# Preparing the slot weights inside the drain of cross attention, with the second pair copied by GpSimd

## The chip, the cores and the metric

The kernel runs on one core of one Trainium2 chip. The metric is the device time of one execution in microseconds (us), lower is better. The program's parts run on TensorE (PE), VectorE (DVE), ScalarE (ACT) and GpSimd (POOL), and SyncE (SP) issues most DMAs.

## The reference

64 sequences of 128 tokens with 128 features go through three sub-layers, each with a residual and a layer norm: self attention, cross attention over 77 context tokens, and a soft mixture of 64 experts with 32 slots each. Only the last one reads what the change touches:

```python
logits = (einsum('tzd,ed->tze', x, phi_w) + phi_b).reshape(t, z, 64, 32)
D = softmax(logits, axis=3)            # over the 32 slots of an expert
C = softmax(logits, axis=2)            # over the 64 experts
X_tilde = einsum('tznp,tzd->npd', D, x)          # gather
X_tilde = tanh(normalise(clip(X_tilde)))
Y_tilde = einsum('npd,ndH->npH', X_tilde, expert_w) + expert_b
Y = einsum('tznp,npH->tzH', C, Y_tilde)          # mix
```

## The kernel before, in words

`decoder_block` runs seven stages one behind the other, each a function with its own block of instruction streams: `setup`, `attention`, `attend_context`, `prepare_slots`, `gather_slots`, `run_experts`, `mix_slots`. A stage begins on every engine after all engines have ended the one before it.

`attend_context` (L380 to L739) takes 64 batches of 128 tokens through a software pipeline, `STEPS = range(-4, B + 4)`. In step n an engine works on batch n (scores), n-1 (exponentials), n-2 (values, sums, division), n-3 (output projection, residual, statistics, normalisation) and n-4 (transposition to `xh` and `xl`). The order of each engine is written out by hand in its loop over STEPS. The steps after B - 1 = 63 are the drain: no new scores, and each step has fewer parts. The names that matter there, by engine:

- PE: `values` L547, `project` L503, `sums` L553, `turn_x2` L508.
- ACT: `exponentials` L596, which reads the four PSUM banks of `psP` (`cross_P`) and raises `e_ready`; the copy to `xh` at L619, which waits for `turn_x2`.
- DVE: `add_residual` L656 to L658, `aggregate` L663, `low_part` L678, `normalise` L668, `invert_sums` L674, `divide` L684.
- POOL: `own_keys` L721, then `normalise` with L727, L730 and L732.

`prepare_slots` (L742 to L791) turns `phi` (2048 slot vectors of 128 features, held with the bias) into the weights of the logits. DVE subtracts from the first 127 features the last one and puts the bias in its place (`diff`, L766 and L769), PE transposes 16 blocks of 128x128 into four PSUM banks (L781), ACT writes the rounded high part `w1h` (L790) and, reordered from (expert, slot) to (slot, expert) and for slots 0 to 15 only, `w2h` (L791), and DVE writes the rests `w1l` (L774) and `w2l` (L775). It works in four chunks of 512 columns. `w1h` and `w1l` are read by the gather stage, `w2h` and `w2l` by the mix stage alone (L1159).

`gather_slots` (L794 to L945) begins with a DMA of the expert weights and one of the expert bias on SP's queue (L837, L838); the stores of kept logits (L841) stand behind them on the same queue, and ACT's `keep` tiles, three of them, are free again when their store has landed (L879). Its steady part takes 128 units, each with L942 and L936 on POOL. `run_experts` (L948 to L1080) begins on DVE with clips (L979), on PE with transposes, and on POOL with nothing until the first statistics are there: L1016 waits for `mv_ready`, L1018 makes `rstd`, and DVE's L994 waits for that. `mix_slots` runs over 64 tiles.

The memory of x1T (the transposed output of self attention, 32 KB in each partition) is kept until the end of `attend_context`; its last reader is the projection of the last pair of batches, `queries_keys` L485, whose semaphore is `qk_made`.

Of the kernel before, what the change touches and what calls it, by code (L numbers as in the profile page):

```python
# [18 lines left out]
ALU = mybir.AluOpType  # L19
# [360 lines left out]
def attend_context(nc, io, w):  # L380
# [4 lines left out]
    with ExitStack() as ctx:  # L385
# [18 lines left out]
        xp = [st.sb(f"xp{i}", [128, 128]) for i in range(2)]  # L404
        halves = nc.dram_tensor("cross_halves", (2, 2, 128, WIDE), F32, kind="Internal").ap()
        psS = st.ps("S", [128, 2, 512])
        psP = st.ps("P", [J, 4, 4, 128])
        psO = st.ps("O", [128, 2, 128])
        psM = st.ps("M", [128, 512])
        QUERY, KEY = slice(0, 256), slice(256, WIDE)  # L410
# [10 lines left out]
        pj_made, y_done, st_done, mv_ready, ve_done, rstd_ready, x2_ready, x2_kept, xT_made, xh_ready, xl_ready = (  # L421
            st.sem(n) for n in ("pj_made", "y_done", "st_done", "mv_ready", "ve_done", "rstd_ready", "x2_ready",
                                "x2_kept", "xT_made", "xh_ready", "xl_ready"))
        pack_set, consts_set, vd_clear, od_set = (st.sem(n) for n in ("pack_set", "consts_set", "vd_clear", "od_set"))
        block = ctx.enter_context(nc.Block())
        PACKS = 6 * 16
# [2 lines left out]
        def is_batch(n):  # L429
            return 0 <= n < B  # L430
# [43 lines left out]
        def _(pe):  # L474
# [75 lines left out]
            def sums(n, part):  # L550
# [4 lines left out]
                if part == 1:  # L555
                    ins.then_inc(av_made, 1)

            for n in STEPS:
                if n == 0:
                    pe.wait_ge(consts_set, 1)  # L560
                if n == 2:
                    pe.wait_ge(od_set, 4)
                if is_batch(n):
                    scores(n, 0)
                for r in projected(n):
                    queries_keys(r)
                for r in valued(n):
                    own_values(r)
                if is_batch(n - 2):
                    values(n - 2, 0)  # L570
                if is_batch(n):
                    scores(n, 1)
                if is_batch(n - 2):
                    values(n - 2, 1)
                if is_batch(n - 3):
                    project(n - 3)
                if is_batch(n - 2):
                    sums(n - 2, 0)
                if is_batch(n - 4):
                    turn_x2(n - 4)  # L580
                if is_batch(n):
                    turned_scores(n)
                    turn_max(n)
                if is_batch(n - 2):
                    sums(n - 2, 1)
                if is_batch(n):
                    shift(n)

        @block.scalar
        def _(act):  # L590
            def exponentials(n, half):
                if half == 0:
                    act.wait_ge(t_made, n + 1)
                    reach(act, av_made, n - 1)
                hs = slice(2 * half, 2 * half + 2)
                ins = act.activation(pT[n % 2][0:J, hs, :, :], psP[:, hs, :, :], ACT.Exp)  # L596
                if half == 1:
                    ins.then_inc(e_ready, 1)

            for n in STEPS:  # L600
                if n == 1:
                    act.wait_ge(od_set, 4)
                if is_batch(n - 1):
                    exponentials(n - 1, 0)
                for r in projected(n):
                    act.wait_ge(qk_made, r + 1)
                    reach(act, stored, 16 * r)
                    act.copy(qk[:, 0, :], psM[:, 0:WIDE]).then_inc(high_ready, 1)
                for r in valued(n):
                    act.wait_ge(v_made, r + 1)  # L610
                    act.wait_ge(vd_clear, 1)
                    reach(act, av_made, 2 * r - 4)
                    act.copy(blocks(vd[r % 3][0:J]), psM[0:J, 0:256].rearrange("j (c h e) -> j c h e", c=8, h=4))\
                        .then_inc(vd_ready, 1)
                if is_batch(n - 1):
                    exponentials(n - 1, 1)
                if is_batch(n - 4):
                    act.wait_ge(xT_made, n - 3)
                    act.copy(w.xh[:, tokens(n - 4)], psM[:, 0:128]).then_inc(xh_ready, 1)  # L619
                if is_batch(n):  # L620
                    act.wait_ge(m_made, n + 1)
                    reach(act, t_made, n)
                    act.copy(mT[:], psM[:, 0:128]).then_inc(mT_ready, 1)

        @block.vector
        def _(dve):
# [54 lines left out]
            def divide(n):  # L681
                dve.wait_ge(rs_ready, n + 1)
                reach(dve, pj_made, n - 1)
                dve.tensor_tensor(oT[n % 2][:], psO[:, 0, :], rs[:], ALU.mult).then_inc(oT_ready, 1)  # L684

            for n in STEPS:
                if n == -3:
                    clear_values()
                if is_batch(n):
                    peak(n, 0)  # L690
                for r in projected(n):
# [5 lines left out]
                    aggregate(n - 3)  # L697
                if is_batch(n - 4):
                    low_part(n - 4)
                if is_batch(n - 3):  # L700
                    normalise(n - 3)
                if is_batch(n - 2):
                    invert_sums(n - 2)
                    divide(n - 2)

        @block.gpsimd
        def _(pool):
# [27 lines left out]
            for n in STEPS:  # L735
                if is_batch(n + 1):
                    own_keys(n + 1)
                if is_batch(n - 3):
                    normalise(n - 3)  # L739


def prepare_slots(nc, w):  # L742

    with ExitStack() as ctx:
        st = Store(nc, ctx, "prep")  # L750
        diff = st.sb("diff", [128, 16, 128])
        psW = st.ps("W", [128, NP])
        diff_done, w_made, wh_done = (st.sem(n) for n in ("diff_done", "w_made", "wh_done"))
        block = ctx.enter_context(nc.Block())

        def by_slot(t, c):

            return t[:].rearrange("d (p n) -> d n p", n=EXPERTS)[:, 16 * c:16 * c + 16, :]

        def by_expert(t, c):  # L760
            return t[:, c * 512:(c + 1) * 512].rearrange("d (n p) -> d n p", n=16)[:, :, 0:MADE]

        @block.vector
        def _(dve):
            dve.wait_ge(w.phi_loaded, 32)
            dve.tensor_copy(diff[:, :, 127], w.bias[:])  # L766
            for c in range(4):
                p = slice(4 * c, 4 * c + 4)
                dve.tensor_tensor(diff[:, p, 0:127], w.phi[:, p, 0:127], w.phi[:, p, 127:128].to_broadcast([128, 4, 127]),  # L769
                                  ALU.subtract).then_inc(diff_done, 1)  # L770
            for c in range(4):
                b = slice(c * 512, (c + 1) * 512)
                dve.wait_ge(wh_done, c + 1)
                dve.tensor_tensor(w.w1l[:, b], psW[:, b], w.w1h[:, b], ALU.subtract)  # L774
                dve.tensor_tensor(by_slot(w.w2l, c), by_expert(psW, c), by_slot(w.w2h, c), ALU.subtract)  # L775

        @block.tensor
        def _(pe):
            for c in range(16):
                pe.wait_ge(diff_done, c // 4 + 1)  # L780
                ins = pe.transpose(psW[:, c * 128:(c + 1) * 128], diff[:, c, :], w.ident)  # L781
                if c % 4 == 3:
                    ins.then_inc(w_made, 1)

        @block.scalar
        def _(act):
            for c in range(4):
                b = slice(c * 512, (c + 1) * 512)
                act.wait_ge(w_made, c + 1)
                act.copy(w.w1h[:, b], psW[:, b])  # L790
                act.copy(by_slot(w.w2h, c), by_expert(psW, c)).then_inc(wh_done, 1)  # L791


def gather_slots(nc, io, w, psX):  # L794
# [153 lines left out]
def run_experts(nc, w, psX):  # L948
# [5 lines left out]
    with ExitStack() as ctx:  # L954
# [55 lines left out]

        @block.gpsimd
        def _(pool):
            for c in range(4):
                p = slice(4 * c, 4 * c + 4)
                pool.wait_ge(mv_ready, c + 1)
# [261 lines left out]
def decoder_block(nc, io, out):  # L1277
    with ExitStack() as ctx:
        st = Store(nc, ctx, "kept")
        w = Weights()  # L1280
        w.xres = st.sb("xres", [128, TOKENS])
        w.xh = st.sb("xh", [128, TOKENS], F32R)
        w.xl = st.sb("xl", [128, TOKENS], F32R)
# [14 lines left out]
        w.bias = st.sb("bias", [128, 16])  # L1298
        with ExitStack() as first:
            sf = Store(nc, first, "first")  # L1300
            w.x1T = sf.sb("x1T", [128, TOKENS])
            w.m, w.w2a, w.b2 = sf.sb("m", [128, 128]), sf.sb("w2a", [128, 129]), sf.sb("b2", [128, 128])
            w.cvec, w.beta = sf.sb("cvec", [128, 1]), sf.sb("beta", [128, 1])
            w.xq, w.xqs, w.xo = sf.sb("xq", [128, 128]), sf.sb("xqs", [128, 128]), sf.sb("xo", [128, 128])
# [4 lines left out]
            w.fill_by_batch, w.fill = fill, fill.rearrange("(r b) t -> r (b t)", b=2)  # L1309
            setup(nc, io, w)  # L1310
            attention(nc, io, w)
            attend_context(nc, io, w)
        w.yk = w.phi
        w.kept = nc.dram_tensor("kept_logits", (TOKENS, 2, SLOTS - MADE, 32), F32, kind="Internal").ap()
        w.w2h, w.w2l = st.sb("w2h", [128, EXPERTS * MADE], F32R), st.sb("w2l", [128, EXPERTS * MADE], F32R)
        with ExitStack() as banks:
            sl = Store(nc, banks, "slots")
            psX = sl.ps("X", [128, 4, 512])
            w.we = sl.sb("we", [128, EXPERTS, 128])
            w.beT = sl.sb("beT", [128, EXPERTS])  # L1320
            with ExitStack() as second:
                ss = Store(nc, second, "second")
                w.w1h, w.w1l = ss.sb("w1h", [128, NP], F32R), ss.sb("w1l", [128, NP], F32R)
                prepare_slots(nc, w)
                gather_slots(nc, io, w, psX)
            run_experts(nc, w, psX)
        mix_slots(nc, w, out)

# [30 lines left out]
```

## Time and profile before

| | us |
|---|---|
| median of 3 runs | 1541.6 |
| lowest and highest run | 1538.96, 1542.17 |
| the profiled execution's own time | 1542.46 |
| its span in the profile | 1540.7 |

| engine | busy us | share of the span |
|---|---|---|
| PE (matmul) | 1395.6 | 91% |
| DVE | 1174.1 | 76% |
| POOL | 1151.4 | 75% |
| ACT | 870.2 | 56% |

The times in the profile count from the span's start. A busy share is an average over stages with different limits, so what matters here is read from the stretches around the change.

### The profile page before, as it was taken

The page shows a single profiled execution, that of the slowest core. Times are in us where ns is not written, and L with a number is a line of the kernel's source. Part 1 is how long each engine was busy: PE and PEld are TensorE (multiplying, and loading weights), DVE is VectorE, ACT ScalarE, POOL GpSimd, SP SyncE. Part 2 cuts the span into 40 slices and gives each one's busy share as a digit, 9 for nine tenths or more (in the row PEclk, how much of TensorE's full clock was granted, in tenths as well). Part 3 has the DMA queues.
Part 4 walks back from the last instruction along what each step waited for, and adds up shares of the span by engine and source line. Part 5 has one row for each costly group of instructions (what it writes and reads, how often), then busy time and mean ns, then how long its engine had stood idle before and what let it go on. Part 6 is the DMA issues. An engine that isn't in the chain of part 4 may idle for free. (4 is left out here: it accounts for less than half of the span.)

```text
span 1540.7 us, 35158 instructions
## 1 busy us (share of the span) xinstructions
PE 1395.6 (91%) x12926; PEld 1111.6 (72%) x12926; DVE 1174.1 (76%) x2389; ACT 870.2 (56%) x1546; POOL 1151.4 (75%) x1028
## 2 busy tenths in 40 slices
PE   5765699999999985999999999996999999999998
PEld 4554466666666653777777777764999999999998
DVE  4898477777777765888888888885788787787885
ACT  3677244444444433667677677662565665656655
POOL 2343466666666642999999999992899999999997
PEclk9897599999999997999999999998999999999999
DMA  5110342323333304222222222211222232232230
GB/s 159 35 35 13 98 118 90 90 90 94 97 94 103 91 19 137 79 80 75 82 77 75 83 76 78 81 69 54 75 87 78 84 94 79 77 93 79 77 93 29
DMA packets 77196, 123.82 MB, mean 80 GB/s; under 512 B 8354, under 2 KB 45795, under 8 KB 77027
## 3 DMA queue, kind: packets, MB, share of 16 engines
q1 hardware_dynamic: 75426, 117.16, 23.9%
q0 software_dynamic: 1088, 4.19, 0.9%
q8 instruction: 104, 1.70, 0.5%
q14 instruction: 66, 0.53, 0.1%
q10 hardware_dynamic: 512, 0.23, 0.1%
HBM read 70.28 MB, written 51.27 MB: 79 GB/s over the span
## 5 line engine op out<-in xcount | busy, mean ns | idle before, releaser
L942 POOL TENSOR_TENSOR gather_d<-gather_e,gather_rinv 128x1024 f32<-128x1024 f32 x128 | 245.0, 1914 | 53.2 <-DVE gather_rinv L921 53.2
L1248 POOL TENSOR_TENSOR mix_c<-mix_e,mix_rinv 128x1024 f32<-128x1024 f32 x128 | 241.0, 1904 | 24.7 <-DVE mix_rinv L1215 24.7
L1175 PEld LDWEIGHTS mix_Y<-kept_phi,mix_cT 128*128 128x128 f32 x2048 | 248.1, 192 | 9.0
L1175 PE MATMUL mix_Y<-kept_phi,mix_cT 128*128 128x128 f32 x2048 | 249.0, 275 | 0.0
L1191 ACT COPY mix_cT<-mix_T 128x1024 f32<-128x1024 f32 x128 | 128.7, 1005 | 170.0 <-PE mix_T L1182 170.0
L1212 DVE TENSOR_REDUCE mix_sums<-mix_e 128x16 f32<-128x1024 f32 x128 | 152.6, 1192 | 85.3 <-ACT mix_e L1195 83.0
L917 DVE TENSOR_REDUCE gather_rsum<-gather_e 128x32 f32<-128x1024 f32 x128 | 156.2, 1220 | 26.9 <-ACT gather_e L890 26.9
L721 POOL TENSOR_TENSOR cross_kd<-cross_pack,kept_consts 128x624 fp32r<-128x624 f32 x128 | 155.3, 1233 | 23.4 <-DMA cross_pack<-cross_halves 23.4
L936 POOL TENSOR_TENSOR gather_dl<-gather_d,gather_dh 128x512 fp32r<-128x512 f32 x128 | 166.1, 1298 | 0.0
L596 ACT ACTIVATE cross_pT<-cross_P 77x1024 f32<-77x1024 f32 x128 | 130.4, 1022 | 48.3 <-PE cross_P L536 48.3
L879 ACT COPY gather_keep<-gather_L 128x256 f32<-128x256 f32 x256 | 94.7, 370 | 105.3 <-PE gather_L L853 98.7
L1182 PE MATMUL mix_T<-kept_consts,mix_c 128*128 128x128 f32 x1024 | 134.6, 275 | 5.1 <-POOL mix_c L1248 5.0
L1259 POOL TENSOR_TENSOR mix_less<-mix_read,mix_high 128x1024 f32<-128x1024 f32 x64 | 122.5, 1915 | 19.5 <-DVE mix_high L1228 19.2
L890 ACT ACTIVATE gather_e<-gather_L 128x1024 f32<-128x1024 f32 x128 | 131.2, 1025 | 8.3 <-PE gather_L L860 1.0
L649 DVE TENSOR_REDUCE cross_mx<-cross_S 128x8 fp32r<-128x624 f32 x128 | 102.9, 804 | 36.8 <-PE cross_S L518 36.7
L867 PE MATMUL slots_X<-gather_d,kept_xres 128*128 128x512 f32 x256 | 130.9, 593 | 0.0
L1182 PEld LDWEIGHTS mix_T<-kept_consts,mix_c 128*128 128x128 f32 x1024 | 117.5, 143 | 6.5 <-POOL mix_c L1248 6.5
L911 DVE TENSOR_REDUCE gather_mx<-gather_L 128x16 fp32r<-128x512 f32 x128 | 88.5, 691 | 33.0 <-PE gather_L L853 24.1
L727 POOL TENSOR_TENSOR cross_veps<-cross_mv,kept_eps 128x1 f32<-128x1 f32 x64 | 12.2, 190 | 128.8 <-DVE cross_mv L663 128.8
L872 PE MATMUL slots_X<-gather_dh,gather_x2h 128*128 128x512 f32 x128 | 101.3, 792 | 2.9 <-DVE gather_x2l L927 1.5
L902 ACT CAST gather_dh<-gather_d 128x512 fp32r<-128x512 f32 x128 | 79.7, 623 | 32.1 <-PE slots_X L874 20.3
L853 PE MATMUL gather_L<-second_w1h,kept_xh 128*128 128x512 f32 x256 | 82.0, 401 | 12.4 <-ACT gather_e L890 8.7
(188 smaller groups left out, 3168.2 us busy)
## 6 DMA issues: line engine op xcount, KB each, us to landing
kept_logits<-gather_keep SPq DMA_DIRECT2D x128, 256.0 KB, 2.0
mix_read<-kept_logits SPq DMA_DIRECT2D x64, 512.0 KB, 3.7
cross_halves<-cross_qk SPq DMA_DIRECT2D x32, 412.0 KB, 3.0
cross_pack<-cross_halves SPq DMA_DIRECT2D x64, 128.0 KB
cross_pack<-cross_halves SPq DMA_DIRECT2D x32, 206.0 KB
cross_pack<-cross_halves SPq DMA_DIRECT2D x64, 78.0 KB
attn_xTg<-in_xT SPq DMA_DIRECT2D x16, 256.0 KB, 2.7
kept_xres<-in_x POOLq DMA_DIRECT2D x4, 1024.0 KB, 12.0
```

The source lines that it names most:

```text
L596: ins = act.activation(pT[n % 2][0:J, hs, :, :], psP[:, hs, :, :], ACT.Exp)
L721: pool.tensor_tensor(kd[n % 2][:, q], keys[:, q].to_broadcast([128, 2, 4, JP]), w.own.unsqueeze(1).unsqueeze(3).to_broadcast([128, 2, 4, J ...
L867: pe.matmul(psX[:, 2 * j + 1, :], w.xres[:, rows(u)], dd[u % 4][:, 1, :], start=first, stop=last)\
L890: act.activation(e[u % 2][:], psL[u % 2][:].rearrange("p i (n s) -> p i n s", n=16), ACT.Exp)\
L917: dve.tensor_reduce(rsum[u % 2][:].rearrange("p (i n) -> p i n", i=2), e[u % 2][:], X, ALU.add)\
L936: pool.tensor_tensor(dl[u % 2][:], dd[u % 4][:, 0, :], dh[u % 2][:], ALU.subtract).then_inc(dl_ready, 1)
L942: pool.tensor_tensor(dd[u % 4][:].rearrange("p i (n s) -> p i n s", n=16), e[u % 2][:], rinv[u % 2][:].rearrange("p (i n) -> p i n", i=2). ...
L1175: ins = pe.matmul(psY[t % 2][:, 0:128], cT[u % 2][:, c, :], w.yk[:, 8 * (u % 2) + c, :], start=(u % 2 == 0 and c == 0), stop=(u % 2 == 1 a ...
L1182: ins = pe.transpose(psT[:, c, :], cc[u % 2][:, 2 * c:2 * c + 2, :], w.ident)
L1191: act.copy(cT[u % 2][:], psT[:]).then_inc(cT_ready, 1)
L1212: dve.tensor_reduce(sums[u % 2][:], e[u % 2][:], X, ALU.add).then_inc(sum_done, 1)
L1248: pool.tensor_tensor(cc[u % 2][:], e[u % 2][:], rinv[u % 2][:].unsqueeze(2).to_broadcast([128, 16, EXPERTS]), ALU.mult)\
```

## The change

The stage `prepare_slots` is gone. Its subtractions, transposes, and the writing of `w1h` and `w1l` are put into the streams of `attend_context`, in steps 63 to 67. The tiles `w1h`, `w1l`, `w2h`, `w2l` and `diff` take the memory of x1T. The transposes write to the four banks of `psP`. `w2h` and `w2l` are no longer made from PSUM by ACT and DVE: POOL copies them, reordered, from `w1h` and `w1l` at the beginning of `run_experts`.

```diff
@@ attend_context @@
-        psP = st.ps("P", [J, 4, 4, 128])
+        banks = st.ps("P", [128, 4, 4, 128])
+        psP = banks[0:J]
+        psW = banks[:].rearrange("d i q t -> d (i q t)")
...
+        diff_done, w_made, wh_done = (st.sem(n) for n in ("diff_done", "w_made", "wh_done"))
@@ tensor @@
+            def turn_weights(c):
+                pe.wait_ge(diff_done, c + 1)
+                pe.wait_ge(e_ready, B)
+                for p in range(4 * c, 4 * c + 4):
+                    ins = pe.transpose(psW[:, p * 128:(p + 1) * 128], w.diff[:, p, :], w.ident)
+                ins.then_inc(w_made, 1)
             for n in STEPS:
...
                 if is_batch(n):
                     shift(n)
+                if n == B:
+                    turn_weights(0)
+                    turn_weights(1)
+                if n == B + 1:
+                    turn_weights(2)
+                    turn_weights(3)
@@ scalar @@
+            def weights_high(c):
+                b = slice(c * 512, (c + 1) * 512)
+                act.wait_ge(w_made, c + 1)
+                act.copy(w.w1h[:, b], psW[:, b]).then_inc(wh_done, 1)
             for n in STEPS:
                 if n == 1:
                     act.wait_ge(od_set, 4)
+                if n == B + 1:
+                    weights_high(0)
+                    weights_high(1)
+                if n == B + 2:
+                    weights_high(2)
+                    weights_high(3)
@@ vector @@
+            def differences(chunks):
+                for c in chunks:
+                    p = slice(4 * c, 4 * c + 4)
+                    dve.tensor_tensor(w.diff[:, p, 0:127], w.phi[:, p, 0:127],
+                                      w.phi[:, p, 127:128].to_broadcast([128, 4, 127]), ALU.subtract)\
+                       .then_inc(diff_done, 1)
+            def weights_low(c):
+                b = slice(c * 512, (c + 1) * 512)
+                dve.wait_ge(wh_done, c + 1)
+                dve.tensor_tensor(w.w1l[:, b], psW[:, b], w.w1h[:, b], ALU.subtract)
             for n in STEPS:
                 if n == -3:
                     clear_values()
+                if n == B + 3:
+                    weights_low(2)
...
                 if is_batch(n - 4):
                     low_part(n - 4)
+                if n == B + 2:
+                    weights_low(1)
                 if is_batch(n - 3):
                     normalise(n - 3)
                 if is_batch(n - 2):
                     invert_sums(n - 2)
                     divide(n - 2)
+                if n == B - 1:
+                    dve.wait_ge(qk_made, PAIRS)
+                    dve.wait_ge(w.phi_loaded, 32)
+                    dve.tensor_copy(w.diff[:, :, 127], w.bias[:])
+                    differences((0, 1))
+                if n == B:
+                    differences((2, 3))
+                if n == B + 1:
+                    weights_low(0)
+                if n == B + 3:
+                    weights_low(3)
@@ prepare_slots: the whole function is removed @@
@@ run_experts, gpsimd @@
+            for low, high in ((w.w1h, w.w2h), (w.w1l, w.w2l)):
+                pool.tensor_copy(high[:].rearrange("d (p n) -> d n p", n=EXPERTS),
+                                 low[:].rearrange("d (n p) -> d n p", n=EXPERTS)[:, :, 0:MADE])
             for c in range(4):
                 p = slice(4 * c, 4 * c + 4)
                 pool.wait_ge(mv_ready, c + 1)
@@ decoder_block @@
-            w.x1T = sf.sb("x1T", [128, TOKENS])
+            w.x1T = x1T_space.enter_context(nc.sbuf_tensor("first_x1T", [128, TOKENS], F32, side="right"))
...
             attention(nc, io, w)
-            attend_context(nc, io, w)
+            x1T_space.close()
+            over = lambda name, shape: ctx.enter_context(nc.sbuf_tensor(f"over_{name}", shape, F32R, side="right"))
+            w.w1h, w.w1l = over("w1h", [128, NP]), over("w1l", [128, NP])
+            w.w2h, w.w2l = over("w2h", [128, EXPERTS * MADE]), over("w2l", [128, EXPERTS * MADE])
+            with nc.sbuf_tensor("over_diff", [128, 16, 128], F32, side="right") as w.diff:
+                attend_context(nc, io, w)
...
-                prepare_slots(nc, w)
-                gather_slots(nc, io, w, psX)
+            gather_slots(nc, io, w, psX)
```

## Rows read from the trace of the kernel before

**Rows 1.** Busy time by stretch; columns: stretch, length, engines, PEclk, DMA share, GB/s.

```profile
584.00:592.00 8.00, 3.49 (x17) 3.28 (x17) 7.11 (x13) 3.85 (x8) 0.00 (x0) 0.71 0.00 0
592.00:598.00 6.00, 6.00 (x14) 4.38 (x14) 1.84 (x3) 1.12 (x3) 0.00 (x0) 0.50 0.74 223
...
611.00:616.00 5.00, 4.85 (x11) 3.51 (x12) 2.86 (x4) 2.29 (x6) 3.13 (x2) 0.58 0.14 52
```

**Rows 2.** Timeline of preparation: start, duration, engine and line, names, count, [idle before].

```profile
584.09 2.47 DVE L769 TENSOR_TENSOR prep_diff<-kept_phi 128x508 f32<-128x508 f32 x4
...
585.98 0.59 ACT L790 CAST second_w1h<-prep_W 128x512 fp32r<-128x512 f32 x1 [2.62 <-PE prep_W L781]
...
590.43 0.71 DVE L774 TENSOR_TENSOR second_w1l<-prep_W,second_w1h 128x512 fp32r<-128x512 f32 x1
591.03 0.62 DVE L775 TENSOR_TENSOR kept_w2l<-prep_W,kept_w2h 128x256 fp32r<-128x256 f32 x1
...
591.99 0.74 SPq L837 DMA_DIRECT2D slots_we<-in_expert_w  x1
```

**Rows 3.** Timeline of cross attention's drain, DVE.

```profile
571.49 0.29 DVE L656 TENSOR_TENSOR cross_y<-cross_M,kept_xres 128x128 f32<-128x128 f32 x1 [1.68 <-PE cross_M L503]
...
576.50 0.29 DVE L656 TENSOR_TENSOR cross_y<-cross_M,kept_xres 128x128 f32<-128x128 f32 x1 [1.68 <-PE cross_M L503]
...
580.40 0.29 DVE L656 TENSOR_TENSOR cross_y<-cross_M,kept_xres 128x128 f32<-128x128 f32 x1 [0.58 <-PE cross_M L503]
...
581.47 0.29 DVE L678 TENSOR_TENSOR kept_xl<-cross_M,kept_xh 128x128 fp32r<-128x128 f32 x1 [0.23 <-ACT kept_xh L619]
...
582.19 0.35 DVE L668 TENSOR_SCALAR cross_xp<-cross_y,cross_mv,cross_rstd 128x127 f32<-128x127 f32 x1 [0.42 <-POOL cross_rstd L730]
...
583.40 0.29 DVE L678 TENSOR_TENSOR kept_xl<-cross_M,kept_xh 128x128 fp32r<-128x128 f32 x1 [0.87 <-ACT kept_xh L619]
```

**Rows 4.** Timeline of the same drain, PE, ACT and POOL.

```profile
572.41 0.19 POOL L727 TENSOR_TENSOR cross_veps<-cross_mv,kept_eps 128x1 f32<-128x1 f32 x1 [3.68 <-DVE cross_mv L663]
...
574.96 1.08 PE L547 MATMUL cross_O<-cross_pT,cross_vd 128*32 128x128 f32 x32 [2.10 <-DVE cross_oT L684]
...
577.33 0.27 ACT L619 CAST kept_xh<-cross_M 128x128 fp32r<-128x128 f32 x1 [4.74 <-PE cross_M L508]
...
579.88 0.49 PE L503 MATMUL cross_M<-first_xo,cross_oT 128*128 128x128 f32 x2 [2.01 <-DVE cross_oT L684]
...
581.17 0.27 ACT L619 CAST kept_xh<-cross_M 128x128 fp32r<-128x128 f32 x1 [3.58 <-PE cross_M L508]
```

**Rows 5.** Timeline of the experts' end, PE: transposes at the full clock.

```profile
1065.17 1.97 PE L1038 MATMUL expert_T<-kept_consts,expert_xt 128*128 128x128 f32 x16 [0.78 <-DVE expert_xt L1006]
```

**Rows 6.** One line's instructions, L927 on DVE: ns min/median/max.

```profile
L927 DVE TENSOR_TENSOR gather_x2l<-kept_xres,gather_x2h x64: 227/228/1305, 604.1 to 1036.4; 128x128 fp32r<-128x128 f32 x64
```

**Rows 7.** Timeline of the gather stage's start, SP's queue and ACT.

```profile
592.78 12.57 SPq L838 DMA_DIRECT2D slots_beT<-in_expert_bT  x1
...
609.80 0.37 ACT L879 COPY gather_keep<-gather_L 128x256 f32<-128x256 f32 x1 [6.18 <-DMA kept_logits<-gather_keep]
```

**Rows 8.** Timeline of the experts' start, DVE and POOL.

```profile
1043.70 2.48 DVE L979 TENSOR_SCALAR expert_xt<-slots_X 128x512 f32<-128x512 f32 x4 [5.95 <-PEq L802]
...
1047.47 0.20 POOL L1016 TENSOR_TENSOR expert_veps<-expert_mv,kept_eps 128x4 f32<-128x4 f32 x1 [5.49 <-DVE expert_mv L988]
...
1048.82 1.36 DVE L994 TENSOR_SCALAR expert_n<-expert_T,expert_mv,expert_rstd 128x128 f32<-128x128 f32 x4 [0.23 <-POOL expert_rstd L1018]
```

**Rows 9.** Groups of POOL's instructions: line, names, shapes, count, busy us, mean ns, idle.

```profile
L942 POOL TENSOR_TENSOR gather_d<-gather_e,gather_rinv 128x1024 f32<-128x1024 f32 x128 | 245.0, 1914 | 53.2 <-DVE gather_rinv L921 53.2
...
L732 POOL TENSOR_SCALAR kept_xres<-cross_y,cross_mv,cross_rstd 128x128 f32<-128x128 f32 x64 | 55.3, 865 | 6.7
...
L713 POOL MEMSET cross_pT<- 64x2048 f32 x2 | 4.0, 2016 | 0.1
```

More of the change, by code:

```diff
@@ L739, in _ @@
                     normalise(n - 3)
[L742 to L791, printed above, removed]
 def gather_slots(nc, io, w, psX):
@@ L1280, in decoder_block @@
         w = Weights()
+        x1T_space = ExitStack()
         w.xres = st.sb("xres", [128, TOKENS])
@@ L1311, in decoder_block @@
             attention(nc, io, w)
-            attend_context(nc, io, w)
+            x1T_space.close()
[4 more added lines that the diff above has]
+                attend_context(nc, io, w)
         w.yk = w.phi
         w.kept = nc.dram_tensor("kept_logits", (TOKENS, 2, SLOTS - MADE, 32), F32, kind="Internal").ap()
-        w.w2h, w.w2l = st.sb("w2h", [128, EXPERTS * MADE], F32R), st.sb("w2l", [128, EXPERTS * MADE], F32R)
         with ExitStack() as banks:
@@ L1320, in decoder_block @@
             w.beT = sl.sb("beT", [128, EXPERTS])
-            with ExitStack() as second:
-                ss = Store(nc, second, "second")
-                w.w1h, w.w1l = ss.sb("w1h", [128, NP], F32R), ss.sb("w1l", [128, NP], F32R)
-                prepare_slots(nc, w)
-                gather_slots(nc, io, w, psX)
+            gather_slots(nc, io, w, psX)
             run_experts(nc, w, psX)
```

## The prediction

> **What bounds the kernel at this place.** I read three views in this order. First the busy time by stretch. Between 584 and 592 us, the whole of `prepare_slots`, no engine has the work of another stage beside it: DVE is busy for 7.11 of 8 us, PE for 3.49, POOL for none [rows 1]. So the stage stands fully in the path, and what shortens the way from the last work of cross attention to the first of the gather shortens the kernel. Second the timeline of this stage and of the drain before it, engine by engine. DVE's last cross instruction starts at 583.40 and ends at 583.69 [rows 3]; DVE's last preparation ends at 591.65, and SP issues the gather's first DMA at 591.99 [rows 2]. From the one to the other: 8.30 us. In the drain the rows' idle times are the room into which the change puts its work. Third the start of the gather, because it decides whether an earlier start is kept. SP's queue is held by the two loads of expert weights for 12.57 us, to 605.35; the stores of kept logits stand behind them, and ACT waits 6.18 us for one of them, until 609.80 [rows 7]. This wait is counted from the moment SP issues the first load, so it moves forward with it. An earlier issue is kept in full; a faster PE before the wait is not worth anything.
>
> **Removed.** The 8.30 us from 583.69 to 591.99.
>
> **Added to the drain, by engine.** *DVE, subtractions.* Four took 2.47 us [rows 2], two take 1.24; with the bias column, of the order of 0.1, the first pair wants 1.35 us and the second 1.24. The first stands behind the division of step 63, in an idle time of 1.68 us before 571.49; the second behind the division of step 64, in one of 1.68 before 576.50 [rows 3]. Cost nothing; without that cover 2.6 us.
>
> *PE, transposes.* Sixteen at the full clock took 1.97 us [rows 5], eight take 1.0. They stand at the end of steps 64 and 65, in idle times of 2.10 us before 574.96 and 2.01 before 579.88 [rows 4]. Their inputs are in time: the second pair of subtractions ends at about 576.1, before the sums of step 65 are done. What they must not overtake, `e_ready` of the last batch, is raised before ACT's idle time of 4.74 us that ends at 577.33 [rows 4]. Cost nothing; uncovered 2.0 us.
>
> *ACT, high parts.* 0.59 us each [rows 2], two per step, 1.2 us. The first two follow the transposes (about 573.9) and lie in the 4.74 us before 577.33; the other two follow those of step 65 (about 578.9) and lie in the 3.58 us before 581.17 [rows 4]. Queued behind them is only the next copy to `xh`, which came later anyway. Cost nothing; uncovered 2.4 us.
>
> *DVE, low parts.* One lasts 0.71 us, and the next queued instruction starts 0.60 after it [rows 2]. Four places. (0) behind the division of step 65, in 0.58 us of idle time before 580.40: nothing, at most 0.1. (1) before the normalisation of batch 63, which had 0.42 us of idle time before 582.19 [rows 3]: 0.60 - 0.42 = 0.18 at most; I take 0.15. Behind it waits the chain normalisation, transposition, `xh`, `low_part`, which ends the stage. (2) in the 0.87 us before 583.40 [rows 3]: nothing. (3) behind the last `low_part`, with nothing to cover it: 0.60 to 0.70. So cross attention's DVE ends at 583.69 + 0.15 + 0.6 to 0.7, about 584.45. The step to the next stage took 591.99 - 591.65 = 0.34 us [rows 2]; SP's first load goes out at 584.8, against 591.99. **Gain of this part: 7.2 us**, between 7.0 and 7.4.
>
> *The port that DVE and POOL share.* One DVE subtraction with both inputs in SBUF took 1305 ns where its median is 228 [rows 6]; in the timeline it began while POOL was in a subtraction of its own. The new DVE subtractions of `diff` have both inputs in SBUF too. They would be held by at most one POOL instruction of 865 ns [rows 9]. But POOL is idle for 3.68 us before 572.41 [rows 4], which holds the first pair, and in the same way before its next batch. The low parts read PSUM and one SBUF tile. I take nothing.
>
> By the Trainium skill (SBUF — State Buffer, Who interferes with whom) a DVE instruction with two SBUF inputs and a GpSimd one that reads SBUF exclude each other for a whole instruction. The 1305 ns agree with it. By this rule a meeting of DVE's `diff` with L732 would cost up to 0.87 us, less the 0.3 to 0.4 us left of the gap, and the order of instructions keeps them apart.
>
> **Moved to POOL.** Two copies of 128x1024 elements between SBUF tiles, reordered on writing (runs of 16 read, written 64 elements apart). No copy on POOL is in the trace. Below: it can't gain, since POOL issues nothing else earlier for it; at the rate of its memset, 2016 ns for 2048 elements [rows 9], one takes 1.0 us. Above: at the rate of L732, 865 ns for 128 elements, 6.9 us. The nearest row is L942, 1024 elements with two inputs, read from and written to SBUF: 1.91 us [rows 9]. A copy has one input fewer, so I take 1.5 us, and 1.9 as its near bound: 3.0 to 3.8 us for both. The cover: the experts' stage starts at 1043.70 and POOL has nothing until 1047.47, 3.77 us [rows 8]. **Cost taken: nothing.** If they last longer, the rest is paid in full: behind them wait L1016 and `rstd`, and DVE's normalisation had only 0.23 us of idle time for it [rows 8]. DVE's instructions beside the copies read PSUM or one small tile, so I expect none of them held.
>
> **Sum.** Profiled execution 1542.46 - 7.2 = 1535.3, a span of 1533.5. The median of the runs is 0.9 below that execution, so I forecast 1541.6 - 7.2 = **1534.4 us**. About 0.2%, 3.1 us, is what a measurement of this kernel can tell from no change.
>
> **The rivals.**
> *Copies beyond their cover* (this is the one on the other side). Place: POOL at the start of the experts; price: what two copies last less 3.77 us. At 3.9 us each the gain falls under 3.1 us, at 5.5 us it is gone, from 7.0 us on the kernel is slower by over 0.2%. At the rate of L732 it is 13.8 - 3.77 = 10.1, for 1544.5. For it: the scattered writing, and that L732 shows how slow POOL can be per element. Against it: L732 has two operations with a scalar for each partition and only 128 elements over which to spread its start, and L942 has 1.87 ns an element. A milder form: the scattered access makes an element half as dear again as in L942, 2.9 us a copy, 2.0 us beyond the cover, for 1536.4; that is the likeliest within this case, 0.07. Chance in all 0.18: 0.09 still faster, 0.06 same, 0.03 slower.
>
> The Trainium skill's GPSIMD Engine Reference (Performance pitfalls for Q7 kernels) has such a rule, which speaks against this part: reading with a step over 8 bytes costs about 2.9 in place of 1.9 cycles per element. The copies read with step 1 and write with a step of 256 bytes, on which the page says nothing, and no row here shows it either way.
>
> *The drain does not hide it.* The waits could chain (DVE's difference late, then the transposes, then the projection of batch 62 or 63 queued behind them on PE). If all of it is paid, 2.6 of subtractions, 2.0 of transposes and DVE's four low parts of 0.6 come to 7.0 us in place of 8.3 us (ACT's high parts beside them, as in the stage itself), a gain of 1.3: 1540.3. Half hidden: 1537.5. For it: gaps of 1.68 us for 1.35 and 0.58 for 0.60 are narrow. Against it: each addition stands behind that step's last instruction and its inputs are a step old. Chance 0.10: 0.03 faster, 0.06 same, 0.01 slower.
>
> *TensorE's clock moves too.* It is at 1.2 GHz throughout the gather's first 6 us and at 0.58 of full on the mean from 611 to 616, when the units resume after the wait for the store [rows 1]; before both PE had been idle. The first stretch costs nothing, since the DMA wait swallows it. The second does: PE is busy for 4.85 us there, and at 2.4 GHz it would be some 2 us less, for 1532.4. The resuming comes after an equal idle time, so I expect the same. Chance 0.04.
>
> **How the numbers follow.** Forecast 0.68, copies 0.18, drain 0.10, clock 0.04. Faster: 0.68 + 0.09 + 0.03 + 0.04 = 0.84; same 0.12; slower 0.04. The range goes down to the clock's case less 0.8 us for the spread of the runs (1542.17 - 1538.96), 1531.6, and up to copies of some 4 us each, 1538.6.
>
> **What would show it.** In the profile after: SP's first load at 584.8; DVE's last low part starting at about 583.7; project of batch 63 still at 579.9 and normalisation within 0.2 us of 582.2; ACT's `keep` wait of about 6 us as before, ending at 602.6; two POOL copies of 1 to 2 us from about 1036.5, and L1016 within 4 us of the experts' start; the stretch from there to the end as long as before. Wrong: a first load later than 585.5 (the drain), a DVE wait for `rstd` over 0.5 us (the copies), a gather or mix stage of another length (what I have not seen).

## The result, and the profile after

Three comparisons were made of the changed kernel with the kernel before. The second and third are among the experiments below (labels e2_after_again and e9_after_third).

| comparison | before, median us | after, median us | ratio, 95% interval |
|---|---|---|---|
| first | 1541.88 | 1529.15 (6 runs, 1528.4 to 1532.79) | 0.9929, 0.9918 to 0.9939 |
| second | 1541.05 | 1531.74 (4 runs) | 0.9944, 0.9927 to 0.9961 |
| third | 1540.88 | 1532.42 (5 runs) | 0.9950, 0.9936 to 0.9964 |

The forecast was 1534.4 in a range of 1531.6 to 1538.6. The gain was 12.7 us in the first comparison, and 9.3 and 8.5 in the others; over all 15 runs the median is 1531.7, against 1541.3 over all 91 of the kernel before, 9.6 us. The direction was right and the size too small: the first result lies some 2.5 us below the range, and the median of all runs 0.1 us inside it.

The first profile of the changed kernel has a span of 1526.9 us in an execution of 1528.72. Its timeline of the drain (start, duration, engine and line, names, count, idle before), which answers to [rows 2 to 4]:

```profile
565.32 1.28 DVE L716 TENSOR_TENSOR over_diff<-kept_phi 128x508 f32<-128x508 f32 x2
...
569.77 1.09 PE L565 MATMUL cross_P<-kept_consts,over_diff 128*128 128x128 f32 x8
...
574.21 1.09 PE L565 MATMUL cross_P<-kept_consts,over_diff 128*128 128x128 f32 x8
...
574.90 1.07 ACT L619 CAST over_w1h<-cross_P 128x512 fp32r<-128x512 f32 x2 [0.89 <-PE cross_P L565]
...
576.16 0.68 DVE L723 TENSOR_TENSOR over_w1l<-cross_P,over_w1h 128x512 fp32r<-128x512 f32 x1
576.29 0.30 PEld L506 LDWEIGHTS cross_M<-first_xo,cross_oT 128*128 128x128 f32 x2 [1.23 <-DVE cross_oT L711]
...
576.82 0.29 DVE L683 TENSOR_TENSOR cross_y<-cross_M,kept_xres 128x128 f32<-128x128 f32 x1
...
578.10 0.68 DVE L723 TENSOR_TENSOR over_w1l<-cross_P,over_w1h 128x512 fp32r<-128x512 f32 x1
...
578.70 0.34 DVE L695 TENSOR_SCALAR cross_xp<-cross_y,cross_mv,cross_rstd 128x127 f32<-128x127 f32 x1
578.95 0.68 DVE L723 TENSOR_TENSOR over_w1l<-cross_P,over_w1h 128x512 fp32r<-128x512 f32 x1
...
579.75 0.29 DVE L705 TENSOR_TENSOR kept_xl<-cross_M,kept_xh 128x128 fp32r<-128x128 f32 x1
579.96 0.68 DVE L723 TENSOR_TENSOR over_w1l<-cross_P,over_w1h 128x512 fp32r<-128x512 f32 x1
...
580.98 0.74 SPq L840 DMA_DIRECT2D slots_we<-in_expert_w  x1
```

The preparation lies in the gaps as forecast: the projection of batch 63 waits for DVE's division alone, the residual starts with no idle time ahead of it, and two low parts stand around the normalisation. From the start of DVE's last `xl` to SP's first load it is 580.98 - 579.75 = 1.23 us, where it was 591.99 - 583.40 = 8.59 [rows 2, 3]. The drain itself got no longer: from the low part of batch 50 to that of batch 63 it is 72.1 us in the kernel before, in a second profile of the changed one (e2) and in one with nothing put into the drain (e7). The other profiles have 72.1 to 74.4 us, with either drain.

The same view at the starts of the gather and of the experts:

```profile
581.77 12.62 SPq L841 DMA_DIRECT2D slots_beT<-in_expert_bT  x1
...
598.80 0.37 ACT L882 COPY gather_keep<-gather_L 128x256 f32<-128x256 f32 x1 [6.48 <-DMA kept_logits<-gather_keep]
...
1031.31 1.97 POOL L1017 CAST over_w2h<-over_w1h 128x1024 fp32r<-128x1024 f32 x1 [1.70 <-SPq L957]
...
1033.15 1.95 POOL L1017 CAST over_w2l<-over_w1l 128x1024 fp32r<-128x1024 f32 x1
...
1035.11 0.20 POOL L1022 TENSOR_TENSOR expert_veps<-expert_mv,kept_eps 128x4 f32<-128x4 f32 x1
...
1036.46 1.37 DVE L997 TENSOR_SCALAR expert_n<-expert_T,expert_mv,expert_rstd 128x128 f32<-128x128 f32 x4 [0.24 <-POOL expert_rstd L1024]
```

From the first load to the end of the DMA wait it is 17.8 us, as before [rows 2, 7]. The two copies take 3.8 us from the first start to the last end. L1022 starts 3.78 us after DVE's first clip, as in the kernel before, where it was 3.77 [rows 8], but without an idle time ahead of it: the copies just fit, with nothing left over.

By stages, us, from the first starts of each in the profiles (the change touches the third and the start of the fifth; e1, e2, e9 and e12 are further profiles of the unchanged files):

| | before | e1 | e12 | after | e2 | e9 |
|---|---|---|---|---|---|---|
| to the end of self attention | 156.9 | 153.2 | 152.8 | 152.5 | 153.2 | 153.0 |
| cross attention to last `xl` | 426.5 | 429.1 | 428.0 | 427.3 | 427.1 | 427.8 |
| `xl` to the first load | 8.6 | 8.6 | 8.6 | 1.2 | 1.2 | 1.2 |
| gather | 451.7 | 452.8 | 452.5 | 450.3 | 450.8 | 450.3 |
| experts | 24.5 | 24.7 | 24.7 | 23.6 | 23.9 | 23.5 |
| mix | 472.5 | 473.0 | 472.8 | 472.0 | 472.6 | 472.3 |

The term of the forecast is there, 7.4 us in every pair. The first profiles differ by 13.8 us, though. The other 6.4, made of 4.4 in self attention, 1.4 in the gather, 0.9 in the experts and 0.5 in the mix, less 0.8 in cross attention, is what the experiments were for.

### The profile page after: what moved, and what is told of

It reads as the page before. It is cut to its first block and busy times, and to the rows that moved or that the text cites. A ratio compares the mean times of both kernels' runs of the same rounds, so it can differ in the third digit from the quotient of the medians.

```text
span 1526.9 us, 35146 instructions
## 1 busy us (share of the span) xinstructions
PE 1387.7 (91%) x12926; PEld 1105.5 (72%) x12926; DVE 1171.2 (77%) x2385; ACT 868.7 (57%) x1542; POOL 1155.0 (76%) x1030
## 5 line engine op out<-in xcount | busy, mean ns | idle before, releaser
L1254 POOL TENSOR_TENSOR mix_c<-mix_e,mix_rinv 128x1024 f32<-128x1024 f32 x128 | 241.0, 1903 | 24.7 <-DVE mix_rinv L1221 24.7
L856 PE MATMUL gather_L<-over_w1h,kept_xh 128*128 128x512 f32 x256 | 82.0, 402 | 10.5 <-ACT gather_e L893 9.0
```

The costliest lines, as they stand in the source:

```text
L1254: pool.tensor_tensor(cc[u % 2][:], e[u % 2][:], rinv[u % 2][:].unsqueeze(2).to_broadcast([128, 16, EXPERTS]), ALU.mult)\
```

## The experiments

**The kernel before again (e1_before_again, no edit).**

> The kernel before, unchanged, so that its stages can be measured in one more execution. The changed kernel's profile was 13.8 us shorter: 4.4 us in self attention (152.5 against 156.9 us to its end), which the change does not touch, 6.5 in the drain and the removed stage, 1.4 in the gather, 0.9 in the experts, 0.5 in the mix. Theory A (the forecast's sum was right for its part, the rest is chance of one execution, by TensorE's clock): the median is 1541 to 1542 and self attention's length differs from 156.9 by one or more us in this execution. Theory B (the rest belongs to the changed kernel, through where its tiles and instructions lie): self attention again ends at 156.9 within 0.5 us and the gather lasts 451.7 within 0.3.

Measured: 1541.09 against 1541.05, ratio 1.0004 (0.9995 to 1.0014). Self attention ended at 153.2 us. The busy time by stretch shows where the first profile had lost its time; the first two rows are the kernel before, the next two e1:

```profile
50.00:60.00 10.00, 7.19 (x44) 5.73 (x42) 7.99 (x28) 6.50 (x24) 3.29 (x3) 0.90 0.10 26
60.00:70.00 10.00, 8.51 (x41) 7.07 (x42) 7.83 (x28) 8.22 (x28) 4.57 (x4) 0.66 0.10 28
```

```profile
50.00:60.00 10.00, 6.28 (x43) 5.12 (x44) 9.52 (x35) 8.21 (x30) 4.56 (x4) 1.00 0.09 26
60.00:70.00 10.00, 6.71 (x48) 5.50 (x48) 9.50 (x38) 8.21 (x28) 3.98 (x5) 1.00 0.19 50
```

The granted clock fell to 1.2 GHz for part of these 20 us in one execution and not in the other, with the same file. Instruction by instruction on ACT, the first profile is 0.2 us behind e1 at 50 us, 3.8 us at 76 us, and 3.7 us at the end of the stage. So 3.7 of the 4.4 us are chance of one execution. The gather and the experts, however, did not get shorter: theory A falls for them. The Trainium skill (TensorE: Matmul & The Clock Gate, Part 1) says that the point at which the clock changes varies between runs of one kernel; these two profiles agree with it.

**The changed kernel again (e2_after_again, no edit).**

> The changed kernel, unchanged, for a second execution of it beside the others. Theory A: self attention's end moves away from 152.5 us, toward a value that the kernel before shows too. Theory B: it is at 152.5 within 0.5 us again, and the gather at 450.3 within 0.3.

Measured: 1531.74 against 1541.05, ratio 0.9944; self attention 153.2, gather 450.8. Self attention bears out theory A, the gather is half way: shorter than in the kernel before, though not within 0.3 of 450.3.

**x1T's place (e3_x1t_right).**

```diff
-            w.x1T = sf.sb("x1T", [128, TOKENS])
+            w.x1T = first.enter_context(nc.sbuf_tensor("first_x1T", [128, TOKENS], F32, side="right"))
```

> The kernel before with one edit: the tile of x1T lies at the other end of the memory, so that every tile allocated after it lies 32 KB lower; no instruction is added or removed. Theory B, by the tiles' place: self attention ends at 152.5 and the kernel is 4 to 5 us faster (1537). Theory A, and B by the instructions' place alone: no change, 1541.5 within 1.5.

Measured: 1540.55, ratio 0.9998 (0.9989 to 1.0007); self attention 153.4. This shift of the tiles does nothing in the first two stages.

**The copies alone (e4_copy_only).**

```diff
 # prepare_slots
-                act.copy(by_slot(w.w2h, c), by_expert(psW, c)).then_inc(wh_done, 1)
...
-                dve.tensor_tensor(by_slot(w.w2l, c), by_expert(psW, c), by_slot(w.w2h, c), ALU.subtract)
 # run_experts, gpsimd
+            for low, high in ((w.w1h, w.w2h), (w.w1l, w.w2l)):
+                pool.tensor_copy(...)
 # decoder_block: w1h and w1l are kept through run_experts
-            run_experts(nc, w, psX)
+                run_experts(nc, w, psX)
```

> One part of the change alone: the preparation keeps its stage, but makes the first pair of weights only, and GpSimd copies the second pair at the experts' start. The removed work is four ACT copies of 0.62 us and four DVE subtractions of 0.62 us; DVE's spacing of a chunk was 1.10 us, of which 0.50 was the second pair, so the stage gets about 2.0 us shorter (DVE then waits for ACT and PE at the stage's clock). The two copies were 1.97 and 1.95 us in the changed kernel and ended as the first statistics came, so they cost nothing. Expected 1539.5 by theory A; by theory B as well, since this part does not move x1T, unless the instructions' place matters.

Measured: 1538.63, ratio 0.9985 (0.9976 to 0.9994), 2.4 us less; the stretch from the last `xl` to the first load 6.8 in place of 8.6 us. The trace puts this part at 1.8 us; the 0.6 more in the medians is within the interval. In this kernel w1h and w1l are also kept until the end of the experts' stage, so that its tiles lie elsewhere.

**The copies twice (e5_copies_twice).**

```diff
-            for low, high in ((w.w1h, w.w2h), (w.w1l, w.w2l)):
+            for low, high in ((w.w1h, w.w2h), (w.w1l, w.w2l), (w.w1h, spare[0]), (w.w1l, spare[1])):
```

> The changed kernel with GpSimd's two copies made twice, the second time into spare tiles that nobody reads. In the changed kernel they last 3.8 us from start to end and the first statistics ask for GpSimd at that very moment. If the cover is used up (theory), all of the further pair is paid: GpSimd's L1022 starts 7.6 instead of 3.8 us after the experts' start, DVE's first normalisation 3.8 later, and the kernel is 3.8 us slower than the changed one (about 1534.5 against 1530.5). Rival: the experts' stage has slack behind, at ScalarE and TensorE, and the kernel loses less than 2 us.

Measured: 1535.38, ratio 0.9964 (0.9951 to 0.9977), 3.7 us over the changed kernel's 1531.7. The timeline at the experts' start:

```profile
1033.36 1.97 POOL L1018 CAST over_w2h<-over_w1h 128x1024 fp32r<-128x1024 f32 x1 [1.69 <-SPq L957]
...
1037.01 1.91 POOL L1018 CAST expert_spare<-over_w1h 128x1024 fp32r<-128x1024 f32 x1
...
1038.78 1.91 POOL L1018 CAST expert_spare<-over_w1l 128x1024 fp32r<-128x1024 f32 x1
...
1040.56 0.20 POOL L1023 TENSOR_TENSOR expert_veps<-expert_mv,kept_eps 128x4 f32<-128x4 f32 x1
...
1041.92 1.37 DVE L998 TENSOR_SCALAR expert_n<-expert_T,expert_mv,expert_rstd 128x128 f32<-128x128 f32 x4 [3.65 <-POOL expert_rstd L1025]
```

L1023 starts 7.20 us after the first copy, 3.4 later than in the changed kernel, and DVE waits 3.65 us for `rstd`. The experts took 27.2 us in place of 23.5 to 23.9. All that is longer than the cover is paid. The further pair adds 3.4 us and not the 3.8 expected, since the copies start 1.8 us apart and last 1.9 to 2.0.

**The preparation behind the drain (e7_prep_behind).** In each of the three streams the calls stand behind the loop over STEPS.

```diff
-                if n == B:
-                    turn_weights(0)
-                    turn_weights(1)
...
+            for c in range(4):
+                turn_weights(c)
...
+            differences(range(4))
+            for c in range(4):
+                weights_low(c)
```

> The changed kernel with the whole preparation behind the drain's last instructions of each engine instead of in its gaps; memory, banks, copies on GpSimd and the missing stage boundary stay. Theory (the drain hid the preparation): the part from DVE's last xl to the gather's first load goes from 1.2 us to about 6.5 us, which is 6.8 us of the kernel with the copies alone less 0.3 for the boundary, and the kernel is 5.3 us slower than the changed one (about 1536). TensorE may do its transposes earlier there, since the drain's differences no longer hold DVE. Rival (most of the gain comes from elsewhere, the places of the tiles and the experts' stage): less than 3 us slower.

Measured: 1537.81, ratio 0.9974 (0.9965 to 0.9983), 6.1 us over the changed kernel's 1531.7; from the last `xl` to the first load 6.3 us in place of 1.2. The drain hides 5.1 us. The other 1.0 of the 6.1 lies outside this stretch; it is of the size by which medians of one kernel differ here.

**The weights' place (e6_weights_right).**

```diff
-        w.w2h, w.w2l = st.sb("w2h", [128, EXPERTS * MADE], F32R), st.sb("w2l", [128, EXPERTS * MADE], F32R)
+        over = lambda name, shape: ctx.enter_context(nc.sbuf_tensor(f"over_{name}", shape, F32R, side="right"))
+        w.w1h, w.w1l = over("w1h", [128, NP]), over("w1l", [128, NP])
+        w.w2h, w.w2l = over("w2h", [128, EXPERTS * MADE]), over("w2l", [128, EXPERTS * MADE])
...
-                w.w1h, w.w1l = ss.sb("w1h", [128, NP], F32R), ss.sb("w1l", [128, NP], F32R)
```

> The kernel before, with the four weight tiles allocated at the end of memory where the changed kernel has them, so that the gather's and the mix's tiles lie where the changed kernel has them; the instructions are the same. In the gather each unit took 3.3866 us in four profiles with the tiles of before and 3.3767 us in two of the changed kernel, over 110 units. Theory P (the place of the tiles does it): 3.377 us here, gather 1.2 us shorter, 1540 against 1541. Rival (the place of the instructions or the preceding stage does it): 3.387 us and no change.

Measured: 1540.12 against 1541.75, ratio 0.9992 (0.9981 to 1.0003), which does not tell 1.2 us from nothing; the trace does. The groups of instructions between 700 and 1000 us, first e1, then e6:

```profile
L942 POOL TENSOR_TENSOR gather_d<-gather_e,gather_rinv 128x1024 f32<-128x1024 f32 x89 | 170.3, 1914 | 19.3 <-DVE gather_rinv L921 19.3
...
L873 PE MATMUL slots_X<-gather_dl,gather_x2h 128*128 128x512 f32 x89 | 35.3, 397 | 0.0
```

```profile
L942 POOL TENSOR_TENSOR gather_d<-gather_e,gather_rinv 128x1024 f32<-128x1024 f32 x89 | 170.4, 1915 | 18.2 <-DVE gather_rinv L921 18.2
...
L873 PE MATMUL slots_X<-gather_dl,gather_x2h 128*128 128x512 f32 x89 | 34.8, 391 | 0.0
```

TensorE's product with `dl` is 6 ns shorter, the others changed by 2 ns at most, and a unit (from the 11th to the 121st start of L942, divided by 110) takes 3.3766 us as in the changed kernel, not 3.3867. Theory P holds: over 128 units the 10 ns are 1.3 us of the gather, which the change gets from where its tiles lie.

**One pair each (e10_w1_right, e11_w2_right).** The same edit for the first pair alone and the second pair alone, one run each.

> The kernel before with the first pair of weights alone at the end of memory: the gather's own tiles lie 16 KB lower, the second pair and the expert weights stay. With all four moved, TensorE's product with the low part of the gather's weights took 391 ns in place of 397 and a unit 3.3766 us in place of 3.3866. If it is the weights' own place or the tiles' shift by 16 KB, the unit is 3.377 us here; if it hangs on the 8 KB of the second pair, it stays 3.387. The time of one run tells nothing at this size.

> The kernel before with the second pair alone at the end of memory: everything of the gather lies 8 KB lower. The counterpart: 3.387 us a unit if the first pair's own place or a shift by 16 KB is what counts, 3.377 if the 8 KB of the second pair do it.

Measured: 3.3766 us and 391 ns with the first pair moved, 3.3866 us and 397 ns with the second:

```profile
L873 PE MATMUL slots_X<-gather_dl,gather_x2h 128*128 128x512 f32 x89 | 34.8, 391 | 0.0
```

```profile
L873 PE MATMUL slots_X<-gather_dl,gather_x2h 128*128 128x512 f32 x89 | 35.3, 397 | 0.0
```

So it is the first pair's place or the 16 KB by which the gather's own tiles (`dl` among them) move, not the 8 KB of the second. Which of these two was not tried.

**The expert weights in pieces (e8_load_in_pieces).**

```diff
-            sync.dma_start(w.we[:], io["expert_w"].rearrange("n d h -> d n h")).then_inc(w.we_loaded, 16)
             sync.dma_start(w.beT[:], io["expert_bT"]).then_inc(w.be_loaded, 16)
             for u in range(UNITS):
+                if u >= 6 and u % 2 == 0 and u < 38:
+                    n = slice((u - 6) * 2, (u - 6) * 2 + 4)
+                    sync.dma_start(w.we[:, n, :], io["expert_w"][n].rearrange("n d h -> d n h")).then_inc(w.we_loaded, 16)
...
-            pe.wait_ge(w.we_loaded, 16)
+            pe.wait_ge(w.we_loaded, 16 * 16)
```

> The changed kernel with the 4 MB of expert weights loaded in 16 pieces, one behind every second store from the seventh unit on, in place of one load ahead of all stores. In the profiles of both kernels ScalarE waits 6.2 and 6.5 us for the store behind that load and the third unit's GpSimd work starts 20.8 us after the load's issue whatever the clock was before. Theory (this wait, not TensorE, sets the gather's start in both kernels): without it the third unit starts at about 15.5 us, two units of 3.4 behind the first at 8.8, and the kernel is 5 us faster than the changed one (about 1525.5). Rival (the start is set by TensorE at its low clock or the pieces slow the stores): 0 to 2 us.

Measured: **1523.65, ratio 0.9885 (0.9870 to 0.9900)**, some 8 us under the changed kernel and 18 under the kernel before. The timeline of the gather's start:

```profile
582.11 0.36 SPq L840 DMA_DIRECT2D slots_beT<-in_expert_bT  x1
...
593.12 1.91 POOL L947 TENSOR_TENSOR gather_d<-gather_e,gather_rinv 128x1024 f32<-128x1024 f32 x1 [1.29 <-DVE gather_rinv L926]
...
596.33 1.92 POOL L947 TENSOR_TENSOR gather_d<-gather_e,gather_rinv 128x1024 f32<-128x1024 f32 x1
```

The third unit's division starts 14.2 us after the stage's first DMA, where it was 20.8 in the changed kernel: 6.6 us, more than the expected 5.3. With the load ahead, the wait for the store was the limit of the gather's start.

The whole gather took 442.0 us, 8.3 less than in the first profile of the changed kernel. The part beyond the 6.6 us lies in the units behind the third: its division and that of the 11th are 26.8 us apart, against 28.3 to 29.0 in the three profiles of the changed kernel. The busy time by stretch shows TensorE's granted clock there, first in the changed kernel, then in e8:

```profile
600.00:606.00 6.00, 5.84 (x17) 4.40 (x18) 3.92 (x5) 3.25 (x8) 3.14 (x2) 0.70 0.12 44
```

```profile
588.00:594.00 6.00, 4.18 (x16) 2.85 (x16) 5.40 (x10) 3.72 (x9) 2.79 (x2) 1.00 0.23 87
594.00:600.00 6.00, 5.34 (x22) 4.09 (x23) 5.33 (x9) 4.23 (x9) 5.93 (x5) 1.00 0.23 87
```

Without the idle stretch the clock did not fall, and the units behind ran at 2.4 GHz. The load's place so cost twice: 6.6 us up to the third unit, and 1.5 to 2.2 in the units behind it, with the low clock that followed the wait. No run removed the one without the other.

**Size and control (e9_after_third, e12_before_third, no edits).**

> The changed kernel once more, with more rounds, to settle its size: the first comparison gave 12.7 us, the second 9.3. By the stages of three profiles of the kernel before (or with its stages) and two of the changed one the difference behind self attention is 10.5 us: 7.4 in the removed stage, 1.5 in the gather, 0.8 in the experts, 0.4 in the mix, 0.4 elsewhere. Theory A (self attention's 152.5 to 156.9 us is chance in both kernels): the medians are 10 to 11 us apart, ratio 0.993. Rival: the changed kernel also shortens self attention, 12 us or more, and its end is under 153.0 us again.

> The kernel before once more, unchanged, as a control of the same size and for one more profile of its stages: median 1541 to 1542, ratio 1.000; self attention's end somewhere between 152.5 and 157 us (theory A), the removed stage 8.6 us, the gather 451.7 to 452.8 us with 3.3866 us a unit, the experts 24.2 to 24.7 us.

Measured: 1532.42, ratio 0.9950 (0.9936 to 0.9964), and 1541.7, ratio 1.0009 (1.0000 to 1.0018). The third comparison gave 8.5 us, under the 10 to 11 of theory A and far from the rival's 12. Self attention was 153.0 and 152.8 us, and 153.4 to 154.9 in the eight experiments with an edit, none of which adds work to that stage: no difference between the kernels is to be seen there, and the rival falls.

These profiles bear on the experts too. Busy time by stretch, the 13th to 16th us of the stage, in the kernel before and in the changed one:

```profile
1056.70:1059.70 3.00, 3.00 (x42) 2.26 (x40) 0.00 (x0) 1.60 (x3) 0.00 (x0) 0.63 0.00 0
```

```profile
1044.30:1047.30 3.00, 2.85 (x59) 2.13 (x61) 0.69 (x1) 1.94 (x4) 0.00 (x0) 1.00 0.00 0
```

The clock is back to 2.4 GHz earlier in the latter. In thirteen profiles (all but e5) the stage's length follows the moment, whichever kernel it is: 23.5 to 23.9 us with the full clock back 12.5 to 13.3 us after the start (after, e2, e9, e6), 24.0 to 24.2 with 13.7 to 14.6 (e10, e7, e4), 24.4 to 24.7 with 15.1 to 15.8 (before, e1, e3, e8, e11, e12). e6 and e8 are the counterexamples to a gain that belongs to the change: the kernel before with 23.8 us, and the changed drain with 24.5.

## Why the prediction was wrong in size

**Right, step by step.** *What bounds.* The stage stood in the path, and the gather's start was set by the load: 17.8 us from load to resumption in both kernels, and 8 us gained once it was out of the way (e8). *Removed and added.* The forecast was 7.2 us (7.0 to 7.4); measured 8.59 - 1.23 = 7.36, with the drain as long as before. The additions on DVE, PE and ACT lay in the gaps named; the last low part alone stood out. Of the 7.4 us, 1.8 are the second pair (8.6 to 6.8, e4) and 5.1 the cover (6.3 to 1.2, e7). The 0.5 between them (6.8 to 6.3) I put down to the stage boundary, which no run took away by itself. *The copies.* Taken at 1.5 us, with 1.9 as near bound; measured 1.97 and 1.95, a little over the near bound, L942's time for two inputs. They cost nothing only because the cover was 3.77 us, and e5 shows the price of going beyond it as the rival had it. *The shared port.* DVE's subtractions took 1.28 and 1.27 us for two, against half of 2.47: nothing was held. POOL was idle during both, so a meeting of the two was not tried.

**Wrong.** The step that failed is the sentence in "What would show it" that the stretch from there to the end would be as long as before. The sum counted only work removed and added, and took the rest of the kernel as fixed. Two things are missing from it.

First, the gather: 1.3 us by the place of its tiles, shown by e6 and e10. The prediction named a gather of another length as a sign of being wrong, but gave it no term. The diff says that the four weight tiles move; I costed that edit at nothing and named no bound for it. 128 units make 10 ns visible.

Second, the clock. The clock's rival had one place, 611 to 616 us, and a chance of 0.04. There it behaved as the forecast said: low again behind the wait. It fell and rose at other points in each execution, though: in self attention (152.5 to 156.9 us over the profiles), in the drain and in the experts (23.5 to 24.7).

The spread was priced too low as well. Six runs of the changed kernel had a median of 1529.15, four and five more had 1531.74 and 1532.42. The three medians lie 3.3 us apart. The range gave the spread 0.8 us, while the two runs that the prediction quotes for it, 1542.17 and 1538.96, are 3.2 apart. Why the first six runs were the fastest stays open, and the mean granted clock does not tell it: runs of the changed kernel at 0.970 took 1528.4 to 1531.93 us, and eleven runs of the kernel before at 0.970 took 1539.57 to 1543.7.

With the pooled 9.6 us, 7.4 are the forecast's term, 1.3 the tiles' place, and the 0.9 left is smaller than this spread. Of the 12.7 us of the first comparison the runs so explain 8.7; the other 4.0 are shown for no part of the change. What of the rest belongs to the change stays open. The mix was 0.5 us shorter in three profiles against three, but 472.9 and 473.3 us in e8 and e5, which have the changed kernel's mix. The experts came out in the short form in all three profiles of the changed kernel, which can be chance or the phase at which it reaches that stage.

**The rivals.** The drain that hides nothing was to give 1540.3; made by hand (e7) it gave 1537.8: 6.3 of the 8.6 us stayed, where the rival let 7.0 of 8.3 stay, and the gather's 1.3 us were gained beside it. The slow copies did not come. The clock's rival priced full clock behind the wait at some 2 us; e8, where the clock stayed up, gained 1.5 to 2.2 us there.

## What to carry to other kernels

A stage in which each engine works alone for a few microseconds is best put into the drain of the stage before it: read each engine's idle time from the timeline, and place the work behind the instruction that precedes the gap; here only the last piece was paid. When an edit moves tiles, repeat the kernel before with the tiles moved and nothing else, since in a loop of a hundred units a few ns each are a result. And look at what the shortened path runs into: here a 4 MB load ahead of small stores on one queue cost some 8 us, nearly as much as the whole stage.

## What the hardware showed that I had not expected

The same TensorE instruction, 128x512 with 128 rows, took 397 or 391 ns depending only on where the tiles of its stage lie, at the same granted clock (1.00 from 700 to 1000 us in all fourteen profiles); the eight profiles with the first pair moved had 391 ns and a unit of 3.3766 or 3.3767 us, the six without had 397 ns and 3.3866 or 3.3867. GpSimd's copy of 1024 elements with one input took 1.91 to 1.97 us, as long as its multiplication of 1024 with two; the elements were written 256 bytes apart, and a dense copy was not tried. And two executions of one file differed by 3.7 us in self attention, in the stretch where the granted clock was low in one of them alone.
